# Grouping the dense weights of a graph kernel by two in four PSUM banks, narrowing its one-hot tiles from 48 to 40 places, and letting gathers run eight batches ahead

## The chip, the cores and the metric

One core of one Trainium2 chip. The metric is the device time of one execution in microseconds; the comparison is between medians of several timed runs. One execution of the kernel before was also recorded by the hardware profiler, and all stretches and durations below come from it.

## The reference

A graph with 3125 nodes of 128 features and 103,125 edges (50,000 drawn ones in both directions and one loop per node), sorted by destination. Two residual blocks follow each other:

```python
x = layernorm(x + gcn(x))        # 3 graph convolutions with elu and skip, then one linear over all 4 states
x = layernorm(x + rgcn(x))

def rgcn(x):                     # the second block
    W = einsum('rb,bio->rio', w_comp, bases)            # 8 relations out of 4 bases
    msg = x[src] * edge_weight[:, None]
    agg = segment_sum(msg, etype * N + dst, 8 * N)      # a sum per relation and node
    return einsum('rni,rio->no', agg.reshape(8, N, -1), W)
```

Only the second block is touched by the change. Since the eight relations are mixed from four bases, the kernel sums each message four times with the four coefficients `edge_weight * w_comp[etype, b]`, and multiplies the four sums of a node by the four bases at the end.

## The kernel before

The first 535 us build the graph's tables and compute the first block; the change does not touch them. What follows is the second block, from about 535 us to the end. It handles the nodes in two ways at once, and both kinds of work are interleaved on TensorE (PE) by a written-out order.

**Gathered part.** 1669 nodes are taken in 14 chunks of up to 128 nodes (c = 0 to 13, the last with 5 nodes). A full chunk has 33 tiles (`TPB`) of 128 edges, in 11 batches of three (`BT`). For each tile POOL issues one indirect DMA that gathers the 128 source rows into `gat` (L837). VectorE (DVE) makes the moving operand `mov`: for 128 edges and 4 bases, a window of `WN` = 48 places of the chunk in which the edge's coefficient stands at its node (`moving`, L1296). PE multiplies the gathered rows by it (`tile`, L1663, fp32, 4 x 48 = 192 columns) and adds to a PSUM bank: bank 0 for the first `HB` = 7 batches, bank 1 for the rest. `mov` has four buffers (`MS`), so DVE is at most four batches ahead of PE. `gat` has a place per tile of a chunk, and POOL waits for tiles of four batches before (`AHEAD`). The indices of the gathers are copied by DVE in three pieces per chunk (`indices`).

**Dense part.** The other 1456 nodes are taken in 13 groups of 112 (h = 0 to 12). For each group a dense weight matrix between all 3125 sources and the 112 nodes is built in 14 octets of 8 nodes (`QD`). For an octet DVE makes two one-hot operands (`hotD` at L1330 and `movD` at L1336, two buffers each, chosen by `k % 2`), PE multiplies them in 24 small matmuls (L1678, 64 rows, 100 columns, two halves of the array in turn, each into its own bank), and ScalarE (ACT) copies the two banks out into `sD` (`evict`, L972). Octets of a group are built eight (`QA`) octets ahead: octets k = 8 to 13 in chunk c belong to group c, k = 14 to 21 to group c + 1. With `sD` complete, 25 products of 448 columns (`dense`, L1684, fp32) run beside the tiles: 18 of group c after tiles 15 to 32 of chunk c, and the other 7 after tiles 0 to 6 of chunk c + 1. The sum stands in bank 5.

**Ends of a chunk.** In chunk c the sums of group c - 1 and chunk c - 1 are multiplied by the bases: ACT copies bank 5 (`copy_dense`, L984), PE runs `finish_dense` (L1697, 8 matmul records) into bank 3 after tile 18, DVE adds the residual and takes mean and variance (`stats_dense`, L1370 to L1373); DVE adds the neighbour's share (`ahead_of`, L1355), PE runs `finish` (L1691) into bank 3 after tile 24, DVE runs `stats` (L1361 to L1364). `lower` and `upper` carry the sums of bank 0 and bank 1 out. ACT takes the roots (`root_dense`, `root`), DVE the norms.

**Order.** Every engine runs its queue strictly in its written order, and the waits name counters: `s_md` (operands of an octet made), `s_sb` (an octet built by PE), `s_se` (a bank of an octet copied), `s_m` (a batch of `mov` made), `s_mu` (a batch of tiles done), `s_df`/`s_dv` (group multiplied / its statistics taken), `s_af` (sum of a chunk complete), `s_fin`/`s_fv` (chunk multiplied / its statistics). DVE's operands for octet k wait until PE has built octet k - 2. On PE an octet waits for the first copied bank of octet k - 1, because the eight banks leave only three for octets (`OCTET_BANKS`).

## Time and profile before

| | |
|---|---|
| median of 3 timed runs | 1131.08 us (1128.03 to 1134.76) |
| the profiled execution, its own time | 1125.61 us |
| its span | 1123.7 us |
| mean granted TensorE clock | 0.965 |
| busy: PE, DVE, ACT, POOL | 92%, 73%, 39%, 45% |
| first and last gather of the second block start at | 536.0 us, 1105.0 us |
| from one chunk to the next (L1702 at 807.67 and 851.32) | 43.65 us |

The program's own time is 1.9 us more than the span. The spread of the three timed runs is 6.7 us. The record of a matmul holds the time in which it drains, so that two records that follow each other overlap: the pace is read from start to start, and a busy PE says only that it has work. In a row that merges several instructions, the second number is the time from the first start to the last end.

### The profile page before, as it was taken

The page shows a single profiled execution, that of the slowest core. Times are in us where ns is not written, and L with a number is a line of the kernel's source. Part 1 is how long each engine was busy: PE and PEld are TensorE (multiplying, and loading weights), DVE is VectorE, ACT ScalarE, POOL GpSimd, SP SyncE. Part 2 cuts the span into 40 slices and gives each one's busy share as a digit, 9 for nine tenths or more (in the row PEclk, how much of TensorE's full clock was granted, in tenths as well). Part 3 has the DMA queues.
Part 4 walks back from the last instruction along what each step waited for, and adds up shares of the span by engine and source line. Part 5 has one row for each costly group of instructions (what it writes and reads, how often), then busy time and mean ns, then how long its engine had stood idle before and what let it go on. Part 6 is the DMA issues. An engine that isn't in the chain of part 4 may idle for free.

```text
span 1123.7 us, 23482 instructions
## 1 busy us (share of the span) xinstructions
PE 1028.7 (92%) x9508; PEld 680.6 (61%) x9508; DVE 816.6 (73%) x1702; ACT 443.5 (39%) x1027; POOL 508.9 (45%) x542
## 2 busy tenths in 40 slices
PE   1578889989999999995799999999999999999997
PEld 1575556656644564464666666666666666666665
DVE  4789899997546556888867777677777667677753
ACT  1598889887200040015423323233233233233320
POOL 5053000000077400000777777677776776776772
PEclk9877999999999999998699999999999999999999
DMA  5253000000111010101422222222222222222221
GB/s 159 51 190 92 1 1 1 1 1 1 58 25 27 8 58 1 44 15 54 118 53 56 58 57 51 55 53 55 55 53 53 57 50 55 55 53 54 58 51 32
DMA packets 48801, 55.34 MB, mean 49 GB/s; under 512 B 15543, under 2 KB 39129, under 8 KB 48182
## 3 DMA queue, kind: packets, MB, share of 16 engines
q0 software_dynamic: 16240, 31.95, 11.4%
q1 hardware_dynamic: 32454, 21.87, 6.8%
q8 instruction: 78, 1.28, 0.5%
q14 instruction: 29, 0.24, 0.1%
HBM read 42.10 MB, written 8.49 MB: 45 GB/s over the span
## 4 chain that ended last, share of the span: by engine, by line
PE 74%; DVE 14%; issue 5%; SPq 2%; ACT 2%; DMA 2%; DVEq 1%; POOL 0%
PE ps L1684 22%; PE ps L1537 20%; PE ps L1663 16%; PE ps L1678 11%; DVE arena L1107 8%; SPq L681 2%; PE ps L1526 1%; PE ps L1691 1%; PE ps L1697 1%; DMA dinv_col<-dinv_scratch 1%; DVE arena L1259 1%; PE ps L1514 1%; DMA arena<-in_dst_dram 1%; PE ps L1484 1%; DVE work L1118 1%
## 5 line engine op out<-in xcount | busy, mean ns | idle before, releaser
L837 POOL DMA_INDIRECT arena<-x_scratch,arena x437 | 412.4, 944 | 185.6 <-issue 110.2
L1537 PE MATMUL ps<-arena,u 125*128 125x480 fp8e5 (+1 forms) x1575 | 358.5, 354 | 1.2 <-ACT arena L891 1.2
L972 ACT COPY arena<-ps 125x400 f32<-125x400 f32 x364 | 169.9, 526 | 375.1 <-PE ps L1678 332.6
L1684 PE MATMUL ps<-arena,u 125*128 125x448 f32 x650 | 297.8, 539 | 0.0
L1663 PE MATMUL ps<-hT,arena 128*128 128x192 f32 x874 | 223.4, 348 | 1.4
L1537 PEld LDWEIGHTS ps<-arena,u 125*128 125x128 bf16 x1575 | 152.5, 97 | 108.1 <-ACT arena L891 1.7
L1663 PEld LDWEIGHTS ps<-hT,arena 128*128 128x128 f32 x874 | 147.4, 190 | 86.0 <-issue 73.3
L1107 DVE TENSOR_TENSOR arena<-arena 128x2048 bf16<-128x2048 bf16 (+2 forms) x158 | 188.8, 1254 | 12.7 <-PE ps L1526 9.5
L1526 PE MATMUL ps<-arena 128*128 128x125 bf16 x1256 | 148.3, 231 | 31.8 <-DVE arena L1107 29.8
L1678 PEld LDWEIGHTS ps<-dinv_all,u 64*128 64x128 bf16 x4368 | 108.8, 96 | 106.3 <-issue 85.6
L1330 DVE TENSOR_TENSOR u<-ps,arena 128x512 bf16<-128x512 bf16 x182 | 76.4, 420 | 111.7 <-PE ps L1678 90.7
L1526 PEld LDWEIGHTS ps<-arena 128*128 128x128 bf16 x1256 | 106.3, 103 | 84.0 <-DVE arena L1107 47.9
L1678 PE MATMUL ps<-dinv_all,u 64*128 64x100 bf16 x4368 | 136.7, 209 | 20.0 <-DVE dinv_all L1336 14.6
L1296 DVE SCALAR_TENSOR_TENSOR hT<-ps,arena 128x192 f32<-128x192 f32 x437 | 154.0, 409 | 0.5
L1336 DVE TENSOR_TENSOR dinv_all<-u,ps 128x1200 bf16<-128x1200 bf16 x182 | 140.0, 769 | 0.0
L1684 PEld LDWEIGHTS ps<-arena,u 125*128 125x128 f32 x650 | 114.8, 190 | 0.0
L811 POOL DMA_INDIRECT arena<-in_dst_dram,wpos x12 | 11.8, 985 | 217.8 <-PE ps L1537 214.4
L891 ACT ACTIVATE arena<-ps,small 128x500 bf16<-128x500 f32 x157 | 109.8, 699 | 0.0
L889 ACT CAST arena<-ps 128x500 fp8e5<-128x500 f32 x157 | 91.5, 583 | 29.8 <-PE ps L1526 28.6
L906 ACT ACTIVATE work<-work 128x480 f32<-128x480 f32 (+1 forms) x21 | 12.2, 580 | 165.7 <-DVE work L1148 165.6
L1146 DVE TENSOR_TENSOR work<-ps,dinv_all 128x480 f32<-128x480 f32 (+1 forms) x21 | 13.0, 621 | 74.8 <-PE ps L1537 74.8
L825 POOL MEMSET work<- 128x512 f32 x1 | 0.5, 525 | 129.1 <-DVE hT L1153 129.1
(187 smaller groups left out, 705.9 us busy)
## 6 DMA issues: line engine op xcount, KB each, us to landing
arena<-x_scratch,arena POOLq DMA_INDIRECT x437, 2.5
arena<-hT SPq DMA_DIRECT2D x2, 1562.5 KB, 7.1
edge_scratch<-arena SPq DMA_DIRECT2D x5, 403.0 KB, 5.2
arena<-in_x_dram SPq DMA_DIRECT2D x1, 1562.5 KB
dinv_all<-dinv_scratch SPq DMA_DIRECT2D x1, 1562.5 KB, 8.8
h_scratch<-hT SPq DMA_DIRECT2D x1, 1562.5 KB, 6.8
first_term_scratch<-arena SPq DMA_DIRECT2D x1, 1562.5 KB
arena<-first_term_scratch SPq DMA_DIRECT2D x1, 1562.5 KB
```

The lines of the kernel that those rows point to most:

```text
L837: nc.gpsimd.indirect_dma_start(out=gat[:, j, :], out_offset=None, in_=x1_d, in_offset=bass.IndirectOffsetOnAxis(ap=idxg[:, j:j + 1], axis= ...
L889: nc.scalar.copy(region[:, :, at:at + GN], ps[:, 3 + k % SLOTS, 0:GN * NBLK].rearrange("p (n s) -> p s n", s=NBLK), saturate=False).then_i ...
L891: nc.scalar.activation(above[k % SLOTS], counts, ACT.Relu, bias=minus7[:, 0:1], accum_out=over[:, k:k + 1]).then_inc(s_adj, 1)
L972: nc.scalar.copy(o, ps[0:BLK, octet_bank(k, w), 0:4 * ND].rearrange("p (i m) -> p m i", i=4)).then_inc(s_se, 1)
L1107: V.tensor_tensor(hot[pair][a][:, 0:GRP * groups, 0:w, :], iota_v[:, None, 0:w, :].broadcast_to([P, GRP * groups, w, 2]), codes[:, :, None ...
L1296: ins = V.scalar_tensor_tensor(mov[:, q % MS, i, :, :], iotaN.broadcast_to([P, NB, WN]), dl[:, ds(c * TPB + (BT * q + i), 1)], coefS[:, :, ...
L1336: V.tensor_tensor(movD[:, k % 2], maskP[:, g:g + 2, None, :, :].broadcast_to([P, 2, NP3, NBLK, 2]), coefQ[:, g:g + 2, :, None, :].broadcas ...
L1526: last = T.matmul(ps[:, 3 + slot, QW * g:QW * (g + 1)], hot[slot // 2][0][:, GRP * (slot % 2) + g, :, h], hot[slot // 2][1][:, GRP * (slot ...
L1537: return T.matmul(ps[:, agg_bank(l, c), 0:CW[c]], u[0:BLK, s, k, :], region[:, s, 0:CW[c]], start=(first and s == 0 and k == 0), stop=(end ...
L1663: last = T.matmul(accN[bank][:, :, a:a + WN], gat[:, j, :], mov[:, q % MS, j % BT, :, :], start=False, stop=False, skip_group_check=True)
L1678: last = T.matmul(ps[:, octet_bank(k, w), ND * i:ND * i + ND].rearrange("p (b v) -> p b v", b=NB), hotD[rows_of, k % 2, g, :, t], cols, st ...
L1684: last = T.matmul(ps[:, 5, 0:NB * DN].rearrange("p (b n) -> p b n", b=NB), xb[0:BLK, s, :], sD[half][0:BLK].rearrange("p (b v) n -> p b v ...
```

## The change

Five things change together in the second block:

- `WN` goes from 48 to 40 places, so a tile has 4 x 40 = 160 columns, in `moving` and in `tile`. `WBACK` goes from 21 to 18 and `SPLIT`/`HB` from 7 batches to 4: bank 0 now takes the first 12 tiles, bank 1 the other 21. `lower` handles 64 places of each base instead of 107, `upper` 100 instead of 68.
- Octets are made and multiplied in pairs, (k, k + 1) with k even, one right behind the other on DVE and on PE. Even octets use banks 2 and 3, odd ones 6 and 7. PE waits with octet k for both banks of octet k - 2.
- Bank 3 being taken, `finish` writes into the unused end of bank 0 (columns 384 to 511), and `finish_dense` into the first 128 columns of bank 5, from which ACT has by then copied the sum of the group (`turned`). Before the first product of the next group overwrites bank 5, PE waits at tile 15 for `stats_dense` (`s_dv`).
- `finish_dense` moves from tile 18 to tile 10, `finish` from tile 24 to tile 15. On DVE `stats_dense` moves from batch 8 to batch 6, `ahead_of` from batch 8 to 7, `stats` and `lower` from batch 9 to 8. ACT's two roots move from octets 18 and 19 to 15 and 16 (`KR`).
- POOL waits for tiles of eight batches before instead of four (`AHEAD`), and the second piece of the next chunk's indices is copied in batch 10 of the chunk before, not in batch 0 of its own.

```diff
-    AHEAD = 4
+    AHEAD = 8
-    KR = QA - (-23 * QD // TPB)
+    KR = QA - (-16 * QD // TPB)
-    WN = 48
-    WBACK = 21
+    WN = 40
+    WBACK = 18
-    SPLIT = (P * BT) * 7 // TPB - WBACK
-    HB = 7
+    SPLIT = (P * BT) * 4 // TPB - WBACK
+    LW = P * (4 * BT - 1) // TPB + WN
+    HB = 4
...
+        def turned(bank):
+
+            return ps[:, bank, 512 - D:512] if bank == 0 else ps[:, bank, 0:D]
-        OCTET_BANKS = ((6, 7), (2, 6), (7, 2))
+        OCTET_BANKS = ((2, 3), (6, 7))
-            return (6, 2)[w] if k % QD == QD - 1 else OCTET_BANKS[k % QD % 3][w]
+            return OCTET_BANKS[k % 2][w]
...
 DVE, in chunk(c, rank):
                         if q == 0:
                             octet(c, QA)
+                            octet(c, QA + 1)
                         moving(c, q, rank == 0)
                         if q == 0 and rank >= 1:
-                            indices(c, 1)
                             upper(c - 1)
                             indices(c, 2)
-                        for k in range(QA + 1, end):
+                        if q == 7 and rank >= 1:
+                            ahead_of(c, HB)
+                        for k in range(QA + 2, end, 2):
                             if STEP.index(k - QA) - 1 in range(BT * q, BT * q + BT):
-                                prepare(c, k)
-                                octet(c, k)
-                        if q == 8 and rank >= 1:
-                            ahead_of(c, HB)
+                                for m in (k, k + 1):
+                                    prepare(c, m)
+                                    octet(c, m)
+                        if q == 6 and rank >= 1:
                             ...
                             stats_dense(c - 1)
-                        if q == 9:
+                        if q == 8:
                             if rank >= 1:
                                 stats(c - 1)
                             ...
                             lower(c)
+                        if q == 10 and following == TPB:
+                            ...
+                            indices(c + 1, 1)
...
 PE, in octet(c, k):
-                    if k >= 1:
-                        pe.wait_ge(s_se, c * (2 * QD) + 2 * k - 1)
+                    if k >= 2:
+                        pe.wait_ge(s_se, c * (2 * QD) + 2 * (k - 1))
...
 PE, in chunk(c, rank, half, following):
                     octet(c, QA)
+                    octet(c, QA + 1)
...
                         if j == DJ:
                             pe.wait_ge(s_se, c * (2 * QD) + 2 * QD)
+                            if rank >= 1:
+                                pe.wait_ge(s_dv, c)
                         if j >= DJ:
                             dense(j - DJ, half)
                         if rank >= 1:
-                            if j == 18:
-                                if rank >= 2:
-                                    pe.wait_ge(s_fv, c - 1)
+                            if j == 10:
                                 finish_dense(c - 1)
-                            if j == 24:
+                            if j == 15:
                                 pe.wait_ge(s_af, c)
-                                pe.wait_ge(s_dv, c)
                                 finish(c - 1)
                         k = QA + STEP[j + 1]
-                        if STEP[j] < STEP[j + 1] < QD and k < end:
+                        if STEP[j] < STEP[j + 1] < QD and STEP[j + 1] % 2 == 0 and k < end:
                             octet(c, k)
+                            octet(c, k + 1)
```

The order on PE in the middle of a full chunk, from the third tile of batch 3 on. `L1663` is a tile, `L1678` an octet's matmuls, `L1684` a product with dense weights, `L1697` finish_dense. Before:

```order
L1663 MATMUL ps<-hT,arena 128x4x48 x2
L1678 MATMUL ps<-dinv_all,u 128x100 [waits octet_copied,dense_moving_ready]
L1678 MATMUL ps<-dinv_all,u 128x100 x23
L1663 MATMUL ps<-hT,arena 128x4x48 [waits moving_ready,gathered4]
L1663 MATMUL ps<-hT,arena 128x4x48 x2
L1678 MATMUL ps<-dinv_all,u 128x100 [waits octet_copied,dense_moving_ready]
L1678 MATMUL ps<-dinv_all,u 128x100 x23
L1663 MATMUL ps<-hT,arena 128x4x48 [waits moving_ready,gathered5]
L1684 MATMUL ps<-arena,u 128x448 [waits octet_copied]
L1663 MATMUL ps<-hT,arena 128x4x48
L1684 MATMUL ps<-arena,u 128x448
```

The same place after; here a tile is `L1674`, an octet `L1689`, a dense product `L1695`, finish `L1702`, finish_dense `L1708`:

```order
L1674 MATMUL ps<-hT,arena 128x4x40
L1708 MATMUL ps<-hT,work 112x128 [waits dense_sum_copied]
...
L1674 MATMUL ps<-hT,arena 128x4x40 [waits moving_ready,gathered4]
L1674 MATMUL ps<-hT,arena 128x4x40 x2
L1689 MATMUL ps<-dinv_all,u 128x100 [waits octet_copied,dense_moving_ready]
L1689 MATMUL ps<-dinv_all,u 128x100 x23
L1689 MATMUL ps<-dinv_all,u 128x100 [waits octet_copied,dense_moving_ready]
L1689 MATMUL ps<-dinv_all,u 128x100 x23
L1674 MATMUL ps<-hT,arena 128x4x40 [waits moving_ready,gathered5]
L1695 MATMUL ps<-arena,u 128x448 [waits dense_variance,octet_copied]
L1702 MATMUL ps<-hT,work 128x128 [waits chunk_sum_ready]
```

Two octets stand together, finish_dense has moved up behind tile 10, and the first dense product behind tile 15 now also waits for `dense_variance`, the statistics that DVE takes of the group before; `finish` follows it at once.

The order on DVE from batch 4 to batch 7 of a full chunk after the change. `L1302` makes a batch of `mov`, `L1336` and `L1342` an octet's operands, `L1376` to `L1379` are stats_dense, `L1361` is ahead_of:

```order
L1336 TENSOR_TENSOR u<-ps,arena 128x512 [waits octet_built]
L1342 TENSOR_TENSOR dinv_all<-u,ps 128x1200
L1302 SCALAR_TENSOR_TENSOR hT<-ps,arena 128x160 [waits tiles_done]
L1302 SCALAR_TENSOR_TENSOR hT<-ps,arena 128x160 x2
L1302 SCALAR_TENSOR_TENSOR hT<-ps,arena 128x160 [waits tiles_done]
L1302 SCALAR_TENSOR_TENSOR hT<-ps,arena 128x160 x2
L1336 TENSOR_TENSOR u<-ps,arena 128x512 [waits octet_built]
...
L1376 TENSOR_TENSOR arena<-ps,dinv_all 112x128 [waits dense_transformed]
...
L1379 BN_AGGR arena<-arena 112x2
L1302 SCALAR_TENSOR_TENSOR hT<-ps,arena 128x160 [waits tiles_done]
L1302 SCALAR_TENSOR_TENSOR hT<-ps,arena 128x160 x2
L1361 TENSOR_TENSOR work<-ps,work 128x4x18 [waits tiles_done]
```

The first two rows are octet 15's operands in batch 4; then come batches 5 and 6 of `mov`, the operands of octets 16 and 17 (the first row of four stands here), and only then stats_dense. Before the change stats_dense stood two batches further on, behind ahead_of.

## Rows read from the trace of the kernel before

**Rows 1.** A window: busy us of PE, PEld, DVE, ACT, POOL; granted clock, DMA.

```profile
700.00:740.00 40.00, 39.91 (x432) 26.54 (x431) 29.76 (x84) 13.12 (x30) 28.40 (x31) 1.00 0.21 54
```

**Rows 2.** Groups by form, 640 to 1050 us: busy us, mean ns of one, idle.

```profile
L1684 PE MATMUL ps<-arena,u 125*128 125x448 f32 x465 | 213.1, 539 | 0.0
...
L1296 DVE SCALAR_TENSOR_TENSOR hT<-ps,arena 128x192 f32<-128x192 f32 x311 | 109.9, 409 | 0.3
...
L1678 PE MATMUL ps<-dinv_all,u 64*128 64x100 bf16 x3182 | 96.4, 205 | 0.0
...
L1691 PE MATMUL ps<-hT,work 128*128 128x128 f32 x72 | 9.5, 275 | 0.0
...
L1355 DVE TENSOR_TENSOR work<-ps,work 128x84 f32<-128x84 f32 x9 | 2.2, 240 | 0.0
```

**Rows 3.** Timeline of PE in one chunk and at the next one's start: start us, length us.

```profile
800.99 0.73 PE L1678 MATMUL ps<-dinv_all,u 64*128 64x100 bf16 x24
801.64 0.59 PE L1663 MATMUL ps<-hT,arena 128*128 128x192 f32 x2
802.07 0.92 PE L1684 MATMUL ps<-arena,u 125*128 125x448 f32 x2
802.83 0.49 PE L1663 MATMUL ps<-hT,arena 128*128 128x192 f32 x2
803.16 0.92 PE L1684 MATMUL ps<-arena,u 125*128 125x448 f32 x2
804.00 0.73 PE L1678 MATMUL ps<-dinv_all,u 64*128 64x100 bf16 x24
...
807.67 0.18 PE L1702 MATMUL ps<-arena 128*128 128x2 bf16 x1
...
822.34 0.72 PE L1678 MATMUL ps<-dinv_all,u 64*128 64x100 bf16 x24
823.18 0.56 PE L1663 MATMUL ps<-hT,arena 128*128 128x192 f32 x2
...
851.32 0.18 PE L1702 MATMUL ps<-arena 128*128 128x2 bf16 x1
```

**Rows 4.** Timeline of DVE: release by an octet, and octet and batch without idle.

```profile
801.83 0.42 DVE L1330 TENSOR_TENSOR u<-ps,arena 128x512 bf16<-128x512 bf16 x1 [0.59 <-PE ps L1678]
...
820.96 0.42 DVE L1330 TENSOR_TENSOR u<-ps,arena 128x512 bf16<-128x512 bf16 x1
...
821.98 1.06 DVE L1296 SCALAR_TENSOR_TENSOR hT<-ps,arena 128x192 f32<-128x192 f32 x3
822.96 0.41 DVE L1330 TENSOR_TENSOR u<-ps,arena 128x512 bf16<-128x512 bf16 x1
```

**Rows 5.** Timeline of DVE: first instruction of stats_dense, and what follows its last.

```profile
1091.10 0.28 DVE L1370 TENSOR_TENSOR arena<-ps,dinv_all 112x128 f32<-112x128 f32 x1
...
1091.85 1.03 DVE L1296 SCALAR_TENSOR_TENSOR hT<-ps,arena 128x192 f32<-128x192 f32 x3
```

**Rows 6.** The gathers' line: counts, starts, idle before, landing; one from the timeline.

```profile
L837 POOL DMA_INDIRECT arena<-x_scratch,arena x437: 938/944/986, 536.0 to 1105.0; - x146
...
  PE ps L1663: 47.4, 76
...
DMA to landing us min/median/max: 2.4/2.5/7.3
...
577.20 0.94 POOL L837 DMA_INDIRECT arena<-x_scratch,arena  x1 [0.30 <-issue]
```

**Rows 7.** Two idle times of PE in the first block, and clocks behind them.

```profile
198.61 0.34 PE L1526 MATMUL ps<-arena 128*128 128x125 bf16 x3 [3.17 <-DVE arena L1107]
...
231.40 0.35 PE L1526 MATMUL ps<-arena 128*128 128x125 bf16 x3 [2.97 <-DVE arena L1107]
...
199.50:202.80 3.30, 3.30 (x21) 2.04 (x19) 2.17 (x3) 2.25 (x5) 0.00 (x0) 0.50 0.02 5
...
231.50:235.00 3.50, 3.50 (x37) 2.42 (x37) 3.38 (x4) 2.51 (x7) 0.00 (x0) 1.00 0.00 0
```

More of the change, by code:

```diff
@@ L57, in build_program @@
     KC = QA - (-DLEFT * QD // TPB)
-    KR = QA - (-23 * QD // TPB)
+    KR = QA - (-16 * QD // TPB)
     NP3 = 3 * NB
     ND = NB * NBLK
-    assert NCHK == DH + 1 and DN == 8 * QD and KC < QD <= KR < QA + QD - 1 and PG <= 6
+    assert NCHK == DH + 1 and DN == 8 * QD and KC < QD <= KR < QA + QD - 1 and PG <= 6 and QA % 2 == 0 and QD % 2 == 0
     PADN = 4095
@@ L242, in build_program @@
         aggD = work[:, 2, 0:NB * DN].rearrange("p (b n) -> p b n", b=NB)
-        accN = [ps[:, k, 0:NB * P].rearrange("p (b n) -> p b n", b=NB) for k in range(3)]
+        accN = [ps[:, k, 0:NB * w].rearrange("p (b n) -> p b n", b=NB) for k, w in enumerate((LW, P, P))]
+        assert LO[HB * BT] >= SPLIT and P - SPLIT + SPILL <= P and NB * LW + D <= 512
+        def turned(bank):
+            return ps[:, bank, 512 - D:512] if bank == 0 else ps[:, bank, 0:D]
         bnst = carve(A_BN, UBT * 8, fp32, 4).rearrange("p (t s) -> p t s", t=UBT)
@@ L1339, in lower @@
                 def lower(c):
-                    V.memset(aggf[:, :, ABOVE:P], 0.0)
-                    V.tensor_tensor(aggf[:, :, 0:ABOVE], accN[0][:, :, AT:P], carry[:, :, 0:ABOVE], ALU.add).then_inc(s_low, 1)
+                    V.memset(aggf[:, :, LW - AT:P], 0.0)
+                    V.tensor_tensor(aggf[:, :, 0:LW - AT], accN[0][:, :, AT:LW], carry[:, :, 0:LW - AT], ALU.add).then_inc(s_low, 1)
                     dve.wait_ge(s_low, c + 1)
@@ L1355, in ahead_of, with stats @@
                     V.tensor_tensor(aggf[:, :, ABOVE:P], accN[0][:, :, 0:AT], aggf[:, :, ABOVE:P], ALU.add).then_inc(s_af, 1)
-                def stats(c, bank=3):
+                def stats(c, bank=0):
                     dve.wait_ge(s_fin, c + 1)
                     yv = ystage[:, 1, :]
-                    link(V.tensor_tensor(yv, ps[:, bank, 0:D], x1r[:, ds(c, 1), :].rearrange("p s d -> p (s d)"), ALU.add))
+                    link(V.tensor_tensor(yv, turned(bank), x1r[:, ds(c, 1), :].rearrange("p s d -> p (s d)"), ALU.add))
                     link(V.bn_stats(fst[:, 0:6], yv))
@@ L1364, in stats, with stats_dense @@
                     V.bn_aggr(fst[:, 6:8], fst[:, 0:6]).then_inc(s_fv, 1)
-                def stats_dense(h, bank=3):
+                def stats_dense(h, bank=5):
                     dve.wait_ge(s_df, h + 1)
                     yv = ystageD[0:DN, 1, :]
-                    link(V.tensor_tensor(yv, ps[0:DN, bank, 0:D], x1rD[0:DN, ds(h, 1), :].rearrange("p s d -> p (s d)"), ALU.add))
+                    link(V.tensor_tensor(yv, turned(bank)[0:DN], x1rD[0:DN, ds(h, 1), :].rearrange("p s d -> p (s d)"), ALU.add))
                     link(V.bn_stats(fstD[0:DN, 0:6], yv))
@@ L1431, in chunk @@
                             lower(c)
+                        if q == 10 and following == TPB:
+                            for b in range(GB[1] // BT, GB[2] // BT):
+                                dve.wait_ge(s_g[b], c * (16 * BT) + 16 * BT)
+                            indices(c + 1, 1)
                         if q == 10 and rank >= 1:
@@ L1446, in _ @@
                 moving(C, 0, False)
-                indices(C, 1, LTILES)
                 upper(C - 1)
@@ L1452, in _ @@
                 stats_dense(DH - 1, 6)
-                stats(C - 1)
+                stats(C - 1, 3)
                 norm_dense(DH - 1, False)
@@ L1687, in dense, with finish, finish_dense @@
                         last.then_inc(s_dp, 1)
-                def finish(c, bank=3):
+                def finish(c, bank=0):
                     for b in range(NB):
-                        last = T.matmul(ps[:, bank, 0:D], aggf[:, b, :], basesS[:, b, :], start=(b == 0), stop=(b == NB - 1))
+                        last = T.matmul(turned(bank), aggf[:, b, :], basesS[:, b, :], start=(b == 0), stop=(b == NB - 1))
                     last.then_inc(s_fin, 1)
-                def finish_dense(h, bank=3):
+                def finish_dense(h, bank=5):
                     pe.wait_ge(s_da, h + 1)
                     for b in range(NB):
-                        last = T.matmul(ps[0:DN, bank, 0:D], aggD[:, b, :], basesS[:, b, :], start=(b == 0), stop=(b == NB - 1))
+                        last = T.matmul(turned(bank)[0:DN], aggD[:, b, :], basesS[:, b, :], start=(b == 0), stop=(b == NB - 1))
                     last.then_inc(s_df, 1)
@@ L1756, in _ @@
                         pe.wait_ge(s_dv, DH - 1)
-                        finish(C - 1)
+                        finish(C - 1, 3)
                 pe.wait_ge(s_af, C + 1)
```

## The prediction

> **What bounds the kernel now.** I read the windows first: in a stretch of 40 us in the second block PE is busy for 39.91 at clock 1.00, POOL for 28.4 and DVE for 29.8 [rows 1]. So PE sets the pace, and what counts is its start-to-start times, read in its timeline [rows 3]: a tile 0.33 (802.83 to 803.16), a dense product 0.76 (802.07 to 802.83), an octet 0.65 (800.99 to 801.64). Ahead of an octet a dense product takes 0.84 instead of 0.76, behind it a tile 0.43 instead of 0.33. So an octet costs 0.65 + 0.08 + 0.10 = 0.83. From chunk to chunk are 43.65 us.
>
> Next comes POOL. A gather is busy for 0.944 and has 0.30 before it, 1.248 from one to the next without a wait, and in the whole block POOL waited only 47.4 us for PE [rows 6]. 33 gathers make 41.2 us: POOL is 2.4 us per chunk behind PE as a bound. Last, DVE's own order: an octet's operands 1.02 (820.96 to 821.98), a batch of moving 0.98 (821.98 to 822.96), 0.11 from the end of an octet on PE to DVE's start (801.73 to 801.83, 800.99 + 0.73 being the end) [rows 3, 4].
>
> **Narrower tiles.** A record of 448 columns takes 539 ns and one of 128 takes 275 [rows 2]: 0.825 ns per column, so 32 columns are 26 ns, and a tile has two records: 0.053 per tile, 0.27 instead of 0.33. 33 tiles: -1.74 us per chunk. For DVE no row shows a width of 160. It saves between nothing and a sixth of 409 ns [rows 2], 0 to 0.07 per instruction; I take the middle, 0.033, so a batch takes 0.88. At nothing the wait below grows by 0.2.
>
> The Trainium skill ("VectorE: DVE Perf Modes", Why PSUM operands drop a tier) says that fp32 from PSUM runs at one element per cycle; by that, 32 elements would save 33 ns. No row here shows the width alone.
>
> **Pairs of octets.** In a pair the second octet has no entry (0.08) and the first no exit. The exit: 0.10 on the tile, and the gap between the last small matmul and the tile. That matmul has 205 ns [rows 2] and ends the 0.73, so it starts at 0.525, and the tile at 0.65 [rows 3]: 0.125, of which 0.02 stays as the step between small matmuls. Per pair 0.08 + 0.10 + 0.105 = 0.29; seven pairs are -2.03 us per chunk. The trace holds no two octets back to back, so the bounds are 0 and 0.29. I take 0.29, since entry and exit appear where the kind of matmul changes, and not between products of 448 and tiles, which both are fp32 over all rows.
>
> The Trainium skill ("TensorEngine Tiling (Array Packing)", Key Properties) says that a change of tiling mode drains TensorE. By that rule the pair saves one drain each way, and the sum would be as I take it; if the gap came with each octet's own waits and bank, it would save nothing (second rival).
>
> **A wait that goes.** The octet at 822.34, in the stretch without dense products, takes 0.84 to its tile instead of 0.65 [rows 3]. I count these 0.19 as gone, since in that stretch PE now comes to operands that are made: -0.2 per chunk.
>
> **The new wait.** PE at tile 15 needs stats_dense, and on DVE this stands behind the operands of octets 16 and 17. Count from the end of octet 12 (behind tile 9) as PE's record has it.
> DVE: release 0.11, octets 14 and 15 2.04, batches 5 and 6 1.76, octets 16 and 17 2.04, stats_dense 0.75 (1091.10 to 1091.85) [rows 5], back to PE 0.06 (estimate, half of the other way): 6.75.
> PE: that record ends 0.18 after the next octet could start, so octet 13 and the exit bring it to -0.18 + 0.53 + 0.23 = 0.58; five tiles 1.36; finish_dense, eight records of 128 columns at 0.11 each, 0.88; entry 0.08, two octets and exit 1.3; tile 15 0.27: 4.5. Octet 14 is ready well before, so nothing of that waits.
> PE stands for 6.75 - 4.5 = 2.25 us. It then has the first dense product (0.76), while DVE makes batch 7 (0.88) and ahead_of (0.16, 240 ns less the overlap [rows 2]) with the hops: finish waits 0.3 more. Together 2.55 per chunk, 11 times (chunks 1 to 11). Queued behind PE's wait are the remaining 18 dense products and all tiles of the chunk, so it is paid in full. Behind DVE's octet 16 stand stats_dense, batch 7 and ahead_of. In chunk 12 no operands of octets 14 to 17 are made, DVE comes early, and the wait is nothing.
>
> **Edits at nothing.** lower and upper (256 elements instead of 428, 400 instead of 272) nearly cancel and stand on DVE while PE works on a chunk. ACT's roots now stand before the copies of octets 16 and 17, and wait for stats in batch 8; octet 19 needs octet 17 copied, and by the same counting this leaves about 1 us. Beyond that each us is paid. AHEAD = 8 and the earlier indices let POOL run on at 41.2 per chunk. PE needs 42.2 (next), so POOL gets ahead by itself and the 47 us in which it waits are no time of PE: nothing, either way. In chunk 1 a gather may come late by about 1 us, since chunk 0 without its first seven products eats POOL's lead; it comes before tile 15 and is taken off the wait there.
>
> **The sum.** Full chunk: -1.74 - 2.03 - 0.2 + 2.55 = -1.4, 42.2 instead of 43.65; 11 of them -15.6. Chunk 0: no new wait, but in its first 15 tiles DVE is the slower engine (now 6.4 operands of 1.02 and five batches of 0.98, 11.4, against PE's 15 x 0.33 + 6.4 x 0.83 = 10.3), so these give only the batches' 5 x 0.1 = 0.5; the other 18 tiles 0.95, four pairs 1.2; the second octet ahead of the first tile takes 0.8: -1.85. Chunk 12: three pairs, no wait: -1.74 - 0.87 - 0.2 = -2.8. Chunk 13, eight tiles: -0.4. Total -20.6. Against the profiled execution's 1125.6 us this is 1105.0; the median shown is 5.5 above that execution, so on the scale of the medians I predict 1131.1 - 20.6 = 1110.5.
>
> **First rival: no stand at tile 15, the gathers bound.** If DVE comes in time, PE would need 43.65 - 4.0 = 39.7 per chunk, below POOL's 41.2. Then the last gather starts at 536.0 + 436 x 1.248 = 1080.1, it lands 2.5 later [rows 6], and two tiles with products and about 10 us of end follow: 1095 on the profile's scale, -29, 1102. For it: POOL is that near. Against it: the counting above has a margin of 2.25 on the wrong side, of which 2 x 2.04 are operands that need octets 12 to 15 built.
>
> **Second rival: the pairs save nothing.** Then 87 pairs (7 in each of chunks 0 to 11, 3 in chunk 12) x 0.29 = 25.2 are missing. But PE comes 0.58 later to tile 15, which takes 6.4 off the wait. -20.6 + 25.2 - 6.4 = -1.8: 1129. Against it: an octet's two waits are long fulfilled in most places and still the entry is 0.08 each time.
>
> **Third rival: the stand costs the clock, and more than all gains.** After an idle time of 3.17 us PE ran at 0.50 for the 3.3 us from 199.50, after one of 2.97 it stayed at 1.00 [rows 7]. The new 2.25 with 0.3 behind it is below both, so mostly not. If a stretch of 3.4 us followed at half speed, it would cost 1.7 per chunk, 19 in 11 chunks: -1.6, 1129.5. If two followed, 3.4 per chunk, 37: +17, 1148, slower. It decides from 20.6 / 11 = 1.9 us lost per chunk.
>
> That the gathers do not in fact run ahead is likely and costs nothing, as worked out.
>
> **How the numbers follow.** Forecast 0.60, with its own range 1104 to 1119: DVE's 0.2 per chunk, half of what the pairs give (9 net of the shorter wait), and the spread of a median, 3 us. Gathers bound 0.13 (1102). Pairs save nothing 0.12 (1129). Clock at half once 0.09 (1129.5), twice 0.06 (1148). The range reaches down past the gathers' case by the spread of a median, to 1099, and up to 1129.5, the second rival's and the third's single case, leaving out the last case and some edges. A difference under 0.5%, 5.7 us, is no change here. Faster than 1125.4: the forecast, the gathers and a part of the second and third rivals, in which the loss is not the whole one: 0.78. Within: 0.15. Slower: 0.07.
>
> **What would show it.** Tile records of about 300 ns, with 0.27 from tile to tile; octets in pairs, 1.1 to 1.2 from the first to the second's end, one entry and one exit; a wait of PE of 2 to 2.6 us at each tile 15 put down to DVE's statistics, eleven times, and a short one before finish; 42.2 us between chunks; POOL with next to no wait for PE; clock 1.00 throughout. It is wrong if the chunk is at 41.2 with PE waiting for gathers, if the pair takes as long as two octets apart, or if the clock row falls below 1.00 after tile 15.

## The result, and the profile after

| | before | after |
|---|---|---|
| median of the timed runs | 1131.66 us (1128.03 to 1134.76, 4 runs) | 1117.75 us (1114.99 to 1120.39, 4 runs) |
| profiled execution, its span | 1125.61, 1123.7 us | 1114.99, 1113.1 us |
| mean granted TensorE clock | 0.965 | 0.954 |
| from the first octet to chunk 0 | 16.0 us | 12.8 us |
| chunks 1 to 11 together | 480.1 us | 476.0 us |
| a full chunk | 43.65 us each time | 42.1 us (3 times), 43.5 to 43.8 us (8 times) |
| chunk 0, chunk 12 | 38.2, 35.9 us | 37.0, 32.7 us |

The ratio of the medians is 0.988 [0.984, 0.992]: the change makes the kernel 13.9 us faster. A second set of runs on another occasion gave the same, 1118.36 us and 0.988 [0.985, 0.991]. The forecast was 1110.5 us, a gain of 20.6, so 6.7 us of it did not come. The chunks say where, since they have two lengths now. (A chunk is counted from the zero product that opens its bank 0, `L1702` before and `L1713` after, to the next chunk's.)

Groups by line for the whole kernel after, which correspond to [rows 2] and [rows 6] (busy us, mean ns of one, idle before and what ended it):

```profile
L843 POOL DMA_INDIRECT arena<-x_scratch,arena x437 | 412.4, 944 | 174.9 <-issue 123.7
...
L1695 PE MATMUL ps<-arena,u 125*128 125x448 f32 x650 | 304.3, 549 | 21.4 <-DVE arena L1379 21.4
...
L1674 PE MATMUL ps<-hT,arena 128*128 128x160 f32 x874 | 193.1, 316 | 3.3 <-DMA arena<-x_scratch,arena 3.2
...
L1302 DVE SCALAR_TENSOR_TENSOR hT<-ps,arena 128x160 f32<-128x160 f32 x437 | 137.2, 373 | 6.6 <-PE ps L1674 6.1
```

`L1695` is the dense product; before, it waited for nothing. Now there are 21.4 us of idle time ahead of it, put down to DVE's last instruction of stats_dense. DVE's instruction for the moving operand (`L1302`) went from 409 to 373 ns.

PE's timeline in chunk 6, which begins at 803.38 and is one of the long ones; it corresponds to [rows 3]:

```profile
804.52 0.44 PE L1674 MATMUL ps<-hT,arena 128*128 128x160 f32 x2
804.80 0.92 PE L1695 MATMUL ps<-arena,u 125*128 125x448 f32 x2
...
807.88 0.92 PE L1695 MATMUL ps<-arena,u 125*128 125x448 f32 x2
808.73 1.28 PE L1689 MATMUL ps<-dinv_all,u 64*128 64x100 bf16 x48
809.94 0.54 PE L1674 MATMUL ps<-hT,arena 128*128 128x160 f32 x2
810.31 0.92 PE L1695 MATMUL ps<-arena,u 125*128 125x448 f32 x2
...
817.98 0.54 PE L1674 MATMUL ps<-hT,arena 128*128 128x160 f32 x2
820.59 0.99 PE L1695 MATMUL ps<-arena,u 125*128 125x448 f32 x2 [2.08 <-DVE arena L1379]
821.49 1.52 PE L1702 MATMUL ps<-hT,work 128*128 128x128 f32 x8
822.80 0.74 PE L1674 MATMUL ps<-hT,arena 128*128 128x160 f32 x2
823.34 1.70 PE L1695 MATMUL ps<-arena,u 125*128 125x448 f32 x2
```

A tile steps on after 0.28 us instead of 0.33 (804.52 to 804.80). A pair of octets takes 1.21 (808.73 to 809.94) where one took 0.65; what it adds to the dense product ahead of it (its entry) is 0.85 - 0.76 = 0.09, and what it adds to the tile behind it (its exit) is 0.37 - 0.27 = 0.10, once for both. Behind the tile at 817.98, tile 15, PE stands for 2.08 us until DVE has the statistics. From start to start it is 2.61 (817.98 to 820.59) instead of 0.27, so the stand costs 2.34: its idle time is counted only from the end of the tile's record, which overlaps what follows it elsewhere. And then the last two rows are longer: a tile's record has 0.74 instead of 0.44, a dense product's 1.70 instead of 0.92.

The same place in chunk 7, a short one:

```profile
861.74 0.54 PE L1674 MATMUL ps<-hT,arena 128*128 128x160 f32 x2
864.35 0.99 PE L1695 MATMUL ps<-arena,u 125*128 125x448 f32 x2 [2.08 <-DVE arena L1379]
865.25 1.16 PE L1702 MATMUL ps<-hT,work 128*128 128x128 f32 x8
866.25 0.44 PE L1674 MATMUL ps<-hT,arena 128*128 128x160 f32 x2
```

The same stand of 2.08 us, and behind it everything at its usual length. The windows of both stretches, and of the one in chunk 5 (busy us and count of PE, PEld, DVE, ACT, POOL; then granted clock, DMA share, GB/s), correspond to [rows 1] and [rows 7]:

```profile
777.80:781.10 3.30, 3.30 (x13) 2.89 (x13) 0.00 (x0) 0.00 (x0) 2.38 (x4) 0.50 0.19 48
822.20:825.50 3.30, 3.30 (x12) 2.48 (x11) 0.00 (x0) 0.00 (x0) 2.40 (x3) 0.50 0.22 55
864.50:867.80 3.30, 3.30 (x17) 2.23 (x18) 0.70 (x3) 0.04 (x1) 2.62 (x3) 1.00 0.25 65
```

The granted clock is 0.50 behind the stands of the long chunks, which is the lower of TensorE's two levels (1.2 GHz), and 1.00 behind those of the short ones. The clock row falls to 0.50 at 603.7, 648.0, 692.4, 777.8, 822.1, 907.5, 951.8 and 1037.2, once in each of the eight long chunks, and in none of the three short ones. The difference from a long to a short chunk is 43.75 - 42.10 = 1.65 us, half of a stretch of 3.3 to 3.4 us, so eight falls cost 13.2.

DVE's timeline up to the stand, which corresponds to [rows 4, 5]:

```profile
813.78 0.42 DVE L1336 TENSOR_TENSOR u<-ps,arena 128x512 bf16<-128x512 bf16 x1 [0.61 <-PE ps L1689]
...
815.83 1.83 DVE L1302 SCALAR_TENSOR_TENSOR hT<-ps,arena 128x160 f32<-128x160 f32 x6
817.58 0.41 DVE L1336 TENSOR_TENSOR u<-ps,arena 128x512 bf16<-128x512 bf16 x1
...
819.62 0.28 DVE L1376 TENSOR_TENSOR arena<-ps,dinv_all 112x128 f32<-112x128 f32 x1
...
820.27 0.18 DVE L1379 BATCH_NORM_AGGREGATE arena<-arena 112x2 f32<-112x6 f32 x1
```

From its release at 813.78 DVE works without a gap: two octets' operands, batches 5 and 6 (1.75 us), two more octets' operands (817.58 to 819.62), and then the statistics. That is the order which the prediction counted.

The gathers' line, which corresponds to [rows 6]:

```profile
L843 POOL DMA_INDIRECT arena<-x_scratch,arena x437: 938/944/988, 537.5 to 1096.0; - x146
...
  DVE arena L1287: 16.3, 7
  PE ps L1674: 7.0, 23
```

POOL waits 7.0 us for PE instead of 47.4. It now waits 16.3 us for indices, seven times, and PE none the longer for it: PE's waits for gathered rows are 3.2 us in the whole kernel, all of them in chunks 0 and 1.

One more stretch has changed, ahead of chunk 0, where octets are built with no tiles between them. PE's timeline there, before and after:

```profile
535.24 1.19 PE L1678 MATMUL ps<-dinv_all,u 64*128 64x100 bf16 x24 [14.57 <-DVE dinv_all L1336]
537.10 1.18 PE L1678 MATMUL ps<-dinv_all,u 64*128 64x100 bf16 x24 [0.68 <-ACT arena L972]
...
551.26 0.61 PE L1702 MATMUL ps<-arena 128*128 128x512 bf16 x1
```

```profile
536.82 2.18 PE L1689 MATMUL ps<-dinv_all,u 64*128 64x100 bf16 x48 [14.55 <-DVE dinv_all L1342]
...
549.63 0.61 PE L1713 MATMUL ps<-arena 128*128 128x512 bf16 x1
```

Before, PE waits about 0.68 us for a copy by ACT ahead of each octet but the first, and nine octets take 16.0 us. After, ten octets in pairs take 12.8, and the waits are for DVE. The stretch is 3.2 us shorter. Part of this can be the clock, since the profile has it at 0.50 through the whole stretch before and through some 9.4 of the 12.8 us after. The stretch itself begins 1.6 us later than before, because the first block, which the change does not touch, ended that much later in this execution.

### The profile page after: what moved, and what is told of

It is laid out like the page before. It is cut to its first block, busy times and chain, and to the rows that moved or that the text cites. A ratio compares the mean times of both kernels' runs of the same rounds, so it can differ in the third digit from the quotient of the medians.

```text
span 1113.1 us, 23493 instructions
## 1 busy us (share of the span) xinstructions
PE 999.8 (90%) x9508; PEld 673.9 (61%) x9508; DVE 800.3 (72%) x1702; ACT 436.9 (39%) x1027; POOL 509.5 (46%) x542
## 3 DMA queue, kind: packets, MB, share of 16 engines
HBM read 42.10 MB, written 8.49 MB: 45 GB/s over the span
## 4 chain that ended last, share of the span: by engine, by line
PE 65%; DVE 20%; issue 6%; DMA 2%; SPq 2%; POOL 2%; ACT 2%; DVEq 1%; ACTq 0%; POOLq 0%
PE ps L1695 22%; PE ps L1548 20%; PE ps L1674 10%; DVE arena L1113 8%; PE ps L1689 7%; DVE dinv_all L1342 3%; POOL arena L843 2%; SPq L687 2%; DVE hT L1302 2%; PE ps L1702 2%; PE ps L1537 2%; DVE u L1336 1%; PE ps L1495 1%; DMA dinv_col<-dinv_scratch 1%; DVE arena L1265 1%
## 5 line engine op out<-in xcount | busy, mean ns | idle before, releaser
L1695 PE MATMUL ps<-arena,u 125*128 125x448 f32 x650 | 304.3, 549 | 21.4 <-DVE arena L1379 21.4
L978 ACT COPY arena<-ps 125x400 f32<-125x400 f32 x364 | 159.7, 527 | 313.4 <-PE ps L1689 288.4
L1674 PEld LDWEIGHTS ps<-hT,arena 128*128 128x128 f32 x874 | 153.5, 195 | 108.5 <-issue 96.3
L1674 PE MATMUL ps<-hT,arena 128*128 128x160 f32 x874 | 193.1, 316 | 3.3 <-DMA arena<-x_scratch,arena 3.2
L1336 DVE TENSOR_TENSOR u<-ps,arena 128x512 bf16<-128x512 bf16 x182 | 76.1, 418 | 142.7 <-PE ps L1689 133.8
L1689 PEld LDWEIGHTS ps<-dinv_all,u 64*128 64x128 bf16 x4368 | 106.1, 95 | 62.1 <-issue 59.2
L1302 DVE SCALAR_TENSOR_TENSOR hT<-ps,arena 128x160 f32<-128x160 f32 x437 | 137.2, 373 | 6.6 <-PE ps L1674 6.1
L1342 DVE TENSOR_TENSOR dinv_all<-u,ps 128x1200 bf16<-128x1200 bf16 x182 | 139.7, 768 | 0.0
L1689 PE MATMUL ps<-dinv_all,u 64*128 64x100 bf16 x4368 | 120.6, 208 | 17.0 <-DVE dinv_all L1342 16.5
L1695 PEld LDWEIGHTS ps<-arena,u 125*128 125x128 f32 x650 | 108.3, 194 | 23.8 <-issue 23.8
```

Of the source, the lines that this page charges most:

```text
L978: nc.scalar.copy(o, ps[0:BLK, octet_bank(k, w), 0:4 * ND].rearrange("p (i m) -> p m i", i=4)).then_inc(s_se, 1)
L1302: ins = V.scalar_tensor_tensor(mov[:, q % MS, i, :, :], iotaN.broadcast_to([P, NB, WN]), dl[:, ds(c * TPB + (BT * q + i), 1)], coefS[:, :, ...
L1342: V.tensor_tensor(movD[:, k % 2], maskP[:, g:g + 2, None, :, :].broadcast_to([P, 2, NP3, NBLK, 2]), coefQ[:, g:g + 2, :, None, :].broadcas ...
L1674: last = T.matmul(accN[bank][:, :, a:a + WN], gat[:, j, :], mov[:, q % MS, j % BT, :, :], start=False, stop=False, skip_group_check=True)
L1689: last = T.matmul(ps[:, octet_bank(k, w), ND * i:ND * i + ND].rearrange("p (b v) -> p b v", b=NB), hotD[rows_of, k % 2, g, :, t], cols, st ...
L1695: last = T.matmul(ps[:, 5, 0:NB * DN].rearrange("p (b n) -> p b n", b=NB), xb[0:BLK, s, :], sD[half][0:BLK].rearrange("p (b v) n -> p b v ...
```

## The experiments

Two theories. **The clock:** the stand at tile 15 costs more than its 2.08 us, because the clock falls behind it in most chunks; with PE kept at work through the stand, every chunk is a short one. **The rival, a matter of place:** the long chunks come from something else in the same stretch (gathers, indices, ACT), and the low clock only goes with it; then work in the stand changes nothing. Beside these I asked whether the stand can be taken away by DVE's order, and where the time then goes. The first four kernels ran on one chip with one set of runs of the kernel before: 1132.44 us.

**The change again.** No edit.

> The changed kernel once more, as the measure for the runs beside it. In its profile eight of the eleven full chunks took 43.7 us and three took 42.1, and the granted clock stood at 0.5 for 3.4 us behind tile 15 in exactly those eight. Theory A (the stand of 2.1 us at tile 15 now and then lets TensorE's clock fall, 1.6 us each time): again chunks of two kinds, 42.1 and 43.7, and 10 to 14 us faster than before. Theory B (the stand and the clock have nothing to do with each other, the slow chunks come from DMA or memory): the two kinds of chunks do not go with the clock rows.

Measured: 1118.36 us (1115.38 to 1119.65), ratio 0.988 [0.985, 0.991]. Stands of 2.08 us again in each chunk from 2 on. The chunks 1 to 11 are 43.8, 43.8, 42.1, 43.8, 42.1, 43.6, 43.8, 42.1, 43.7, 43.8, 42.1: seven long ones, and the clock row falls to 0.50 in these seven and in no other. Which chunks are hit differs from the first trace, what a hit costs does not.

**Work in the stand.** Nine products with operands of zeros, which add nothing to bank 1, right ahead of the wait at tile 15:

```diff
                         if j == DJ:
                             pe.wait_ge(s_se, c * (2 * QD) + 2 * QD)
                             if rank >= 1:
+                                for _ in range(9):
+                                    T.matmul(ps[:, 1, 0:512], zeros[:, 0:P], zeros[:, 0:512], start=False, stop=False, skip_group_check=True)
                                 pe.wait_ge(s_dv, c)
```

> Nine products of zeros (512 columns each, about 0.22 us, added to bank 1 where they change nothing) are put on PE directly ahead of its wait at tile 15. PE still goes on only when DVE's statistics come, so the work behind comes no earlier, but PE is busy while it stands. Theory A (clock): no clock row of 0.5 behind tile 15, every full chunk 42.1 us, about 13 us less than the changed kernel, 1105 on the scale of before at 1131.7. Theory B (something else makes the eight chunks slow): chunks of 43.7 stay, no gain. Theory C (zeros do not count as work for the clock): clock rows of 0.5 stay as well.

Measured: 1109.27 us (1107.95 to 1111.41), ratio 0.981 [0.978, 0.984], 9.1 us less than the change beside it. PE's timeline in chunk 6:

```profile
816.70 0.54 PE L1674 MATMUL ps<-hT,arena 128*128 128x160 f32 x2
817.29 1.89 PE L1734 MATMUL ps<-arena 128*128 128x512 bf16 x8
819.23 1.02 PE L1695 MATMUL ps<-arena,u 125*128 125x448 f32 x2
820.22 1.16 PE L1702 MATMUL ps<-hT,work 128*128 128x128 f32 x8
```

Eight of the nine products have a record; the weight loads of all nine are there (108 in 12 chunks). The first dense product still comes 2.53 us behind tile 15 (2.61 in the change), so DVE is waited for as before, but PE works meanwhile. The windows from 600 to 1090 us, of this kernel and of the change beside it:

```profile
600.00:1090.00 490.00, 487.99 (x5423) 333.54 (x5435) 340.63 (x976) 149.50 (x348) 368.19 (x391) 1.00 0.22 57
```

```profile
600.00:1090.00 490.00, 467.16 (x5292) 326.71 (x5291) 340.21 (x972) 149.70 (x350) 360.95 (x383) 0.98 0.21 56
```

The clock stays at 1.00, the first of the 11 chunks takes 42.4 us and the others 42.1 or 42.2. They are 11.0 us shorter together (463.5 against 474.5), where 7 x 1.65 = 11.6 were due. Chunk 12 is 1.9 longer (34.8 against 32.9): it has no stand, and there the nine products are plain extra work. 11.0 - 1.9 = 9.1, as the medians differ; the two traces' spans differ by 10.5, of which 1.4 arose ahead of chunk 1. So the clock is shown and the rival of place falls. The "about 13" that I expected was too much mostly by these 1.9 us and by counting eight falls where the change beside it had seven.

**The statistics a batch earlier on DVE.** stats_dense in batch 5, ahead of octets 16 and 17, not behind them; ahead_of stays in batch 7:

```diff
+                        if q == 5 and rank >= 1:
+                            ...
+                            stats_dense(c - 1)
                         if q == 7 and rank >= 1:
                             ahead_of(c, HB)
...
-                        if q == 6 and rank >= 1:
-                            ...
-                            stats_dense(c - 1)
```

> On DVE stats_dense moves from behind the operands of octets 16 and 17 (batch 6) to batch 5; ahead_of stays behind batch 7. The wait for the statistics at tile 15 goes, but finish needs ahead_of one product later. Theory 1 (DVE's whole row of work up to ahead_of is the bound, 6.75 + 1.1 us after octet 12): the stand moves from the first dense product to finish, 2.1 to 2.4 us, chunk unchanged at 42.1 where the clock holds; in all within 5 us of the changed kernel. Theory 2 (only the statistics were late): the stand falls to under 0.5, the chunk to 41.2, bound by POOL's 33 gathers, and the time by 20 us or more.

Measured: 1119.69 us (1113.16 to 1124.17), ratio 0.989 [0.985, 0.993], no different from the change. A row of its waits (us in total, times, longest), and its PE timeline in chunk 6:

```profile
PE ps L1702 <- DVE work L1361: 21.1, 12, 2.2
```

```profile
822.36 0.54 PE L1674 MATMUL ps<-hT,arena 128*128 128x160 f32 x2
822.73 0.92 PE L1695 MATMUL ps<-arena,u 125*128 125x448 f32 x2
825.88 1.16 PE L1702 MATMUL ps<-hT,work 128*128 128x128 f32 x8 [2.23 <-DVE work L1361]
```

The wait for the statistics is gone, and the next one, `finish` for ahead_of, which was about 0.15 us when it followed the first, is now 2.23. It is about as long as the old one because ahead_of still stands behind octets 16 and 17 and a batch. Seven chunks are long again, with the clock at 0.50 in each of them. Moving one statement forward gains no more than the time until the next wait that rests on the same engine.

**Both sums earlier.** As the last experiment, and ahead_of in batch 6:

```diff
-                        if q == 7 and rank >= 1:
+                        if q == 6 and rank >= 1:
                             ahead_of(c, HB)
```

> As the run before, and ahead_of moves from batch 7 to batch 6, ahead of the operands of octets 16 and 17 too. Now nothing that PE needs at tile 15 stands behind those operands. If PE's work and the stand were all (39.6 us of work per chunk), the gathers become the bound: 33 x 1.248 = 41.2 us per chunk, waits of PE for gathers in place of those for DVE, spread out, last gather near 1081 us in the profile; 1125.6 - 27 = about 1098 on the profile's scale, 1104 as a median, and the clock at 1.00 if no single wait for gathers is over 2 us. A rival: the two operands of octets 16 and 17, now 0.9 us later, make PE wait at tile 18 instead; then the chunk stays over 41.5 and the wait is at the octet.

Measured: 1104.01 us (1099.55 to 1105.59), ratio 0.975 [0.972, 0.978]. This beats both kernels: 28 us less than before, 14 less than the change. Its waits from 580 to 1090 us, its gathers' line, and PE's timeline at tile 15 of chunk 6 and at one place of chunk 12:

```profile
POOL arena L843 <- issue: 122.2, 401, 0.3
...
PE ps L1674 <- DMA arena<-x_scratch,arena: 17.3, 13, 2.5
```

```profile
L843 POOL DMA_INDIRECT arena<-x_scratch,arena x437: 940/944/987, 545.0 to 1089.3; - x146
...
  PE ps L1674: 2.4, 8
```

```profile
815.94 0.54 PE L1674 MATMUL ps<-hT,arena 128*128 128x160 f32 x2 [1.19 <-DMA arena<-x_scratch,arena]
816.31 0.92 PE L1695 MATMUL ps<-arena,u 125*128 125x448 f32 x2
817.07 1.05 PE L1702 MATMUL ps<-hT,work 128*128 128x128 f32 x8
...
1063.11 0.90 PE L1674 MATMUL ps<-hT,arena 128*128 128x160 f32 x2 [2.17 <-DMA arena<-x_scratch,arena]
```

No wait for DVE is left at tile 15, and PE now waits for gathered rows, mostly once a chunk. The gathers run from 545.0 to 1089.3 at 544.3 / 436 = 1.248 us each, without a pause worth naming: this is the prediction's first rival, brought about by two more moves on DVE. The chunks take 39.6 to 44.0 us, 41.3 in the mean (454 us for 11), against 41.2 for 33 gathers. The one at 44.0 had a wait of 2.49 us for a gather at 649.9 and the clock at 0.50 from 653.4; the gathers went on meanwhile, so the next two chunks took 39.6 and 39.8. The waits of 0.7 to 2.0 us in chunks 3 to 11 had no such sequel. In chunk 12 one of 2.17 us had it again: the clock is at 0.50 from 1063.0 (the last row).

**The parts apart, twice.** These were meant to price 40 places without pairs, pairs without 40 places, and the eight batches of lead. The edits, on the kernel before (the first), on the change (the second) and on the version just shown (the others):

```diff
tiles_40_only, on the kernel before:
-    WN = 48
-    WBACK = 21
+    WN = 40
+    WBACK = 18
pairs_with_48 and stats_5_sum_6_with_48:
-    WN = 40
-    WBACK = 18
+    WN = 48
+    WBACK = 21
stats_5_sum_6_ahead_4:
-    AHEAD = 8
+    AHEAD = 4
```

> The kernel before with 40 places per tile instead of 48 (and 18 places of reach back instead of 21) and nothing else: single octets in three banks, finish in bank 3, gathers four batches ahead. Theory 1 (the tile's price is 0.053 us, with no new stand): 43.65 - 1.74 = 41.9 us per chunk plus small waits for DVE, 42.0, clock 1.00; 1132.4 - 20 = 1112, faster than the changed kernel as a whole (1118). Theory 2 (the narrow tile only pays together with the rest): less than 10 us.

> The changed kernel with 48 places per tile again (reach back 21): pairs, banks, the new order and eight batches ahead alone. Per chunk -2.0 us for the pairs, -0.2, and the stand at tile 15: DVE has 0.1 more per batch, PE 0.05 more per tile, so 2.1 to 2.4 us, and 0.3 before finish: 43.7 to 43.9 where the clock holds, no change against before. With TensorE's clock falling behind the stand in some 8 of 11 chunks, 1.6 each: +13, so 1145, slower than before (1132). A rival: the pairs give their 2 us on top of what the stand takes, chunks of 42 and a time of 1115.

> The kernel with stats_dense in batch 5 and ahead_of in batch 6 (1104.0), with 48 places per tile. If it is the gathers that bound this version (33 x 1.248 = 41.2 us per chunk), PE's work of 39.6 + 1.74 = 41.35 per chunk is only just above, waits for gathers nearly vanish, and the time stays within 3 us of 1104: the narrow tile is worth next to nothing there. If PE's own work bounded it, 33 tiles x 0.053 x 13 = 23 us would be added: 1127.

> The same version with AHEAD = 4 in place of 8. If POOL issues its gathers without a pause anyway, since PE is never four batches behind it, nothing changes: 1104, within 2 us. If the longer lead is what lets POOL run through (POOL would wait for PE in the stretches in which PE has dense products, and miss that time where PE has none), the chunk grows by a part of a us and the time by 5 to 10 us.

In these runs every kernel was slower, the kernel before too: 1313.49 us (17 runs, 1306.36 to 1325.48) in place of 1132.44 on the same chip eleven minutes earlier. So all four ran a second time on another chip:

> The kernel before with 40 places per tile and nothing else, once more, since in its first job every kernel, the one before included (1313 instead of 1132), was slowed by stops of PE within octets. Theory 1 (the tile's price is 0.053 us, with no new stand and no loss of clock): 42.0 us per chunk, clock 1.00, 20 us less than before, so 1112 where before is 1132, and faster than the whole change (1118). Theory 2 (the narrow tile only pays together with the rest): less than 10 us.

> The changed kernel with 48 places per tile again, once more for the same reason. Chunks of 43.7 to 43.9 where the clock holds, 1.6 more where it falls behind the stand; if that is in some 8 of 11 chunks, 13 us slower than before, 1145. A rival: chunks of 42 and 1115.

> Statistics in batch 5 and the sum in batch 6, with 48 places per tile, once more. If the gathers bound this version (41.2 us per chunk; PE's work would be 41.35): within 3 us of the version with 40 places (1104.0 beside a before of 1132.4), few waits for gathers. If PE's work bounded it: 23 us more.

> The same version with 40 places and AHEAD = 4, once more. If POOL is never four batches ahead of PE there, nothing changes (ratio to before 0.975, within 0.002). If the longer lead carries POOL through, 5 to 10 us more.

| kernel | first time, ratio to before | second time, ratio to before |
|---|---|---|
| before | 1313.49 us | 1313.06 us |
| tiles_40_only | 1309.75 us, 0.997 [0.994, 1.000] | 1309.32 us, 0.998 [0.995, 1.000] |
| pairs_with_48 | 1469.91 us, 1.121 [1.116, 1.126] | 1469.97 us, 1.119 [1.115, 1.123] |
| stats_5_sum_6_with_48 | 1432.19 us, 1.089 [1.085, 1.094] | 1437.83 us, 1.093 [1.087, 1.099] |
| stats_5_sum_6_ahead_4 | 1342.86 us, 1.023 [1.020, 1.027] | 1298.91 us, 0.989 [0.986, 0.993] |

Rows of PE, ACT and DVE in the second trace of tiles_40_only show what is different:

```profile
1099.67 0.73 PE L1678 MATMUL ps<-dinv_all,u 64*128 64x100 bf16 x24 [1.28 <-ACT arena L972]
1100.34 0.81 PE L1663 MATMUL ps<-hT,arena 128*128 128x160 f32 x4
1105.50 1.19 PE L1678 MATMUL ps<-dinv_all,u 64*128 64x100 bf16 x24 [4.35 <-ACT arena L972]
```

```profile
1104.86 0.92 ACT L972 COPY arena<-ps 125x400 f32<-125x400 f32 x2 [4.49 <-remote]
```

```profile
1104.86 0.42 DVE L1330 TENSOR_TENSOR u<-ps,arena 128x512 bf16<-128x512 bf16 x1 [3.17 <-remote]
```

PE ended an octet at 1099.67 + 0.73 = 1100.40 and had only two tiles behind it before the next octet. ACT and DVE, which wait for that octet, both started at 1104.86, some 4.5 us later, where [rows 4] have 0.11. "Remote" says that the profile knows no instruction of this core as the releaser. PE then waited 4.35 us for ACT. The same wait of ACT summed up (us in total, times, longest), in this trace and in the second one of pairs_with_48:

```profile
ACT arena L972 <- remote: 246.6, 57, 6.9
```

```profile
ACT arena L978 <- remote: 351.7, 46, 14.8
```

With pairs the late starts are fewer and longer (7.6 us each in the mean against 4.3). Whether the signal came late or PE really ended the octet late, the trace does not tell, since the ends of matmuls are modelled. So these eight runs price how a version bears such delays, not what 40 places, pairs or the lead are worth in the runs of the comparison; the change as it stands was not run in these conditions, and nothing of the prediction is judged by them. What caused the delays, and the worth of each part by itself, stay open. The sizes of the parts below come from the rows of the undisturbed traces alone.

## Why the prediction was right, and where not

**The bound.** Right: PE set the pace, POOL was next at 1.248 us per gather, and the version with both sums earlier ran into exactly that.

**Narrower tiles.** 0.053 per tile was forecast; the step went from 0.33 to 0.27 or 0.28. DVE's instruction was to save 33 ns and saved 36 (409 to 373). The Trainium skill ("VectorE: DVE Perf Modes", Why PSUM operands drop a tier) caps fp32 from PSUM at the plain rate, by which 32 elements are an estimated 33 ns. The trace is within 3 ns of that.

**Pairs.** 0.29 per pair was forecast, and 0.29 came. By the means of all starts in six chunks before, two octets apart cost 2 x (0.656 + 0.093 + 0.100) = 1.70; a pair costs 1.21 + 0.09 + 0.10 = 1.40. The second octet has no entry and no gap of its own, so the second rival, in which pairs save nothing, is refuted by the row. The Trainium skill says that a change of tiling mode drains TensorE ("TensorEngine Tiling (Array Packing)", Key Properties). The trace agrees in that the extra time stands only where the kind of matmul changes, but the number type changes there too: behind the one zero product over all rows (`L1702`, bf16) a tile also takes 0.41 instead of 0.33. So which of the two costs the time stays open.

**The wait that was to go.** It went: every last octet of a pair takes 0.65 to its tile, the one without dense products beside it too.

**The new wait.** 2.25 was forecast, as what DVE's order takes less what PE's takes from start to start. Counted in the same way the rows have 2.34 (2.61 less a tile's 0.27): DVE took 6.92 instead of 6.75, with 0.14 for the way back to PE where 0.06 was estimated, and PE 4.58 instead of 4.5. The 2.08 in brackets is the idle time alone. The stand came eleven times, in chunk 1 partly as a wait for a gather (1.37 at 601.3, then 0.64), as the prediction also had it. The short wait before `finish` was forecast at 0.3; the rows have 0.14 of it at 865.25 (0.90 behind the product instead of 0.76). So the two come to 2.48 instead of 2.55.

**The sum of the terms.** With the sizes as measured, -33 x 0.054 - 7 x 0.29 - 0.2 + 2.48 = -1.53 per chunk, and 43.65 - 42.10 = 1.55 was measured where the clock held (42.2 was forecast for the chunk). Without the falls of the clock 11 chunks would be 17.3 us shorter (15.6 forecast). Chunk 0 gave 1.2 instead of 1.85, with 1.8 us of waits for gathered rows in it; chunk 12 gave 3.2 instead of 2.8, chunk 13 and the end 0.4 as forecast. Together 22.1 against 20.6. A slip that changes little: the second rival counts 87 pairs, the sum itself 84.

**A term that the sum left out.** The octets ahead of chunk 0 are built in pairs and in other banks too, and the prediction gave them nothing, without a reason. That stretch is 3.2 us shorter.

**The clock: the step that failed.** The prediction took the new 2.25 us as "below both" idle times of [rows 7], "so mostly not", and gave a fall once per chunk 0.09. It priced the fall at 1.7; it cost 1.65, in 8 of 11 chunks, 13.2 us. Of the gains this leaves 22.1 + 3.2 - 13.2 = 12.1; the first block, which the change does not touch, ended 1.6 us later in after's execution; together the 10.6 by which the spans differ, to rounding. The medians differ by 13.9, because the profiled execution of before lay 6.1 us below its median and that of after 2.8 below its own. The error was in reading two idle times (3.17 with a fall, 2.97 without) as a threshold between them. They only showed that the outcome can go either way there, and the very same 2.08 us of idle time then went both ways within one trace. With eleven such stands in a row, the question was how many would be followed by a fall, not whether. The clock row below 1.00 behind tile 15 is one of the signs of being wrong that the prediction itself had named.

**The edits at nothing.** POOL's longer lead and the earlier indices took 40 us out of POOL's waits for PE. PE's own waits for gathered rows are 3.2 us in all, so nothing shows that this moved PE, as forecast; that the lead matters once PE is faster could not be tried undisturbed.

So the forecast's mechanisms in the chunks were right in place and close in size, and on top of them the third rival, in its case of one stretch, came true in eight of eleven chunks. That the number was 7 us off and not 12 owes something to luck: the 3.2 us ahead of chunk 0 and the 1.5 us by which the other terms came out larger stood against the 13.2 of the clock.

## What to carry to other kernels

When an edit gives TensorE a recurring stall of about two microseconds, price it with and without a half-speed stretch behind it; here 2.08 us of idle time cost 2.34 in steps and in most chunks 1.65 more for the clock, and filling it with products of zeros gave the latter back. Before a wait is moved, look for the next wait that rests on the same engine's order: both have to move, as the pair of experiments on DVE's statistics and sum shows. When a rotation of buffers changes, follow it into every stretch that uses it, the start-up too. And when the waits between two engines are gone, look for what now runs without a pause: here the gathers, at 1.248 us each, set 41.2 us per chunk.

## What the runs showed of the hardware that was not expected

- The granted clock fell to 0.50 behind an idle time of 2.08 us in 8 of 11 chunks of one trace and 7 of 11 of another, with the same instructions around it, while [rows 7] have one of 2.97 us behind which it stayed at 1.00. In both traces single chunks are spared, after one to three falls; in that of the statistics in batch 5, with stands of 2.23 us, the first two chunks are spared in a row. In chunk 1 of the first two traces the fall came with two waits of 1.4 and 0.6 us and of 1.3 and 0.8 us, half a microsecond apart. Why some are spared is open.
- Products whose operands are all zeros, put into the stand, kept the clock at 1.00 in all eleven chunks.
- In the later runs, on two chips, ACT and DVE started up to 4.5 us behind the end of PE's octet in the rows shown where 0.11 is usual, and the kernel before took 16% longer. Of the 189 us between the spans of tiles_40_only there and of before here (1312.9 and 1123.7), only 22 had arisen where the first block's last linear begins (525.1 instead of 503.0); the rest came in the second block. What it was is not known.
